# A graph network on one core: in the edge-maximum passes, every fourth block of edges comes by products with one-hots instead of every fifth

## What is computed

```python
def _sage_pool_layer(x, src, dst, Wp, bp, Ws, Wn, b, n_nodes):
    m = jax.nn.relu(x @ Wp + bp)
    msgs = m[src]
    agg = jax.ops.segment_max(msgs, dst, num_segments=n_nodes)
    agg = jnp.where(jnp.isfinite(agg), agg, 0.0)
    return x @ Ws + agg @ Wn + b
```

## Time and profile before

| | |
|---|---|
| median of 3 runs | 2809.11 us (2801.65 to 2812.70) |
| the profiled execution | 2804.64 us, its span 2802.9 us |
| first maximum pass, GpSimd's part | 663 to 1173 us |
| second maximum pass, GpSimd's part | 1246 to 1762 us |
| propagation (L2405) | 2000 to 2796 us |

### The profile page before, as it was taken

One profiled execution on the slowest core, in us unless ns is written; L12 is line 12 of the kernel. 1 busy time (PEld: TensorE's weight loads), 2 busy tenths in 40 slices (PEclk: granted clock), 3 DMA queues, 4 the chain that ended last, 5 costly groups with the idle time before them and its releaser, 6 DMA issues. The chain is left out here.

```text
span 2802.9 us, 72099 instructions
## 1 busy us (share of the span) xinstructions
PE 2456.9 (88%) x29232; PEld 1982.7 (71%) x29232; DVE 1763.4 (63%) x4833; ACT 1156.4 (41%) x2585; POOL 1299.8 (46%) x1607
## 2 busy tenths in 40 slices
PE   6998999986879888677889887469899999999999
PEld 3666777764556555445556655369899999999998
DVE  6997999986778877446768776320444444444444
ACT  5997888874434444424434444310311111111110
POOL 4007999974888888558888887410000000000000
PEclk8558999997999999789989998569999999999999
DMA  5103000013555555534545555549200000000000
GB/s 165 42 2 102 12 13 13 13 50 97 143 124 141 137 131 135 126 96 122 130 117 150 128 137 143 146 161 348 84 2 2 1 2 2 2 2 2 2 2 19
DMA packets 147170, 227.40 MB, mean 81 GB/s; under 512 B 55568, under 2 KB 112619, under 8 KB 146162
## 3 DMA queue, kind: packets, MB, share of 16 engines
q1 hardware_dynamic: 120350, 184.69, 22.0%
q0 software_dynamic: 22944, 36.72, 6.7%
q10 hardware_dynamic: 3540, 1.30, 0.2%
HBM read 122.26 MB, written 100.35 MB: 79 GB/s over the span
## 5 line engine op out<-in xcount | busy, mean ns | idle before, releaser
L1892 POOL DMA_INDIRECT max_row<-table,max_src_rows x640 | 670.5, 1048 | 181.7 <-issue 165.9
L1934 PE MATMUL max_far<-adj 128*96 128x512 f16 x1800 | 538.6, 401 | 7.7 <-issue 5.8
L2060 DVE TENSOR_SCALAR adj<-adj,node_numbers 128x512 f16<-128x512 f16 x900 | 325.0, 370 | 210.8 <-PE max_far L1934 129.2
L1758 POOL TENSOR_SCALAR e<-e 128x512 f32<-128x512 f32 (+1 forms) x625 | 365.7, 604 | 178.5 <-ACT e L1746 160.9
L2405 PE MATMUL prop<-g,adj 128*128 128x192 f16 x4608 | 387.2, 247 | 8.5 <-DVE g L2479 8.5
L1772 DVE TENSOR_TENSOR e<-e,a_ps 128x1024 f32<-128x1024 f32 (+1 forms) x313 | 372.3, 1195 | 32.6 <-PE a_ps L1684 12.6
L2405 PEld LDWEIGHTS prop<-g,adj 128*128 128x128 f16 x4608 | 380.7, 98 | 13.4 <-issue 9.2
L2405 PE MATMUL prop<-weights_then_states,adj 128*128 128x192 f16 x4608 | 384.3, 246 | 0.0
L2405 PEld LDWEIGHTS prop<-weights_then_states,adj 128*128 128x128 f16 x4608 | 378.9, 98 | 3.7 <-issue 2.5
L1746 ACT ACTIVATE e<-s_ps 128x512 f32<-128x512 f32 (+1 forms) x625 | 335.5, 585 | 60.2 <-PE o_ps L1696 37.8
L2513 DVE SCALAR_TENSOR_TENSOR support_parts<-prop,coef,weights_then_states 128x96 f32<-128x96 f32 x384 | 120.6, 314 | 303.9 <-PE prop L2405 226.0
(11 more groups left out here) (292 smaller groups left out, 3702.5 us busy)
## 6 DMA issues: line engine op xcount, KB each, us to landing
weights_then_states<-weights SPq DMA_DIRECT2D x100, 400.0 KB, 4.8
weights<-max_rows_w SPq DMA_DIRECT2D x52, 400.0 KB
rows_dram<-max_out SPq DMA_DIRECT2D x100, 192.0 KB
weights<-adj SPq DMA_DIRECT2D x48, 400.0 KB
max_same<-same_dram SPq DMA_DIRECT2D x196, 96.0 KB
rows_dram<-adj SPq DMA_DIRECT2D x96, 192.0 KB
max_row<-table,max_src_rows POOLq DMA_INDIRECT x640
adj<-ids_dram SPq DMA_DIRECT2D x36, 128.0 KB
```

Of the source, the lines that this page charges most:

```text
L1758: nc.gpsimd.tensor_scalar(e_tile(u), e_tile(u), math.exp(10.0), math.exp(-10.0), ALU.min, ALU.max).then_inc(clipped, 1)
L1892: nc.gpsimd.indirect_dma_start(row[i % RING][:, j, :], None, table_dram, bass.IndirectOffsetOnAxis(ap=src_rows[:, 4 * n + j:4 * n + j + 1] ...
L1934: mm = nc.tensor.matmul(far_ps[j % 2][0:D, :], parts[:, k, a, :], hot[(T * j + k) % HOTS], start=k == a == 0, stop=k == T - 1 and a == 1)
L2060: nc.vector.tensor_scalar(hot[i % HOTS], ids[j % 2], numbers[:, k:k + 1], None, ALU.is_equal).then_inc(hot_made, 1)
```

## The change

`FAR` is `range(4, 92, 4)` instead of `range(5, 92, 5)`. The far blocks are now 4, 8, ... 88: 22 instead of 18, and 76 near blocks instead of 80. Nothing else is edited; all that follows comes from loops over `FAR`, `near` and `far_tiles`.

```diff
 AWAY, NEAR_END = 5, 3
 
-FAR = range(5, 92, 5)
+FAR = range(4, 92, 4)
 
 K_PROP = 16
```

## The result

The changed kernel takes 2777.2 us as the median of four runs (2772.0 to 2783.7), beside 2805.5 us for the kernel before in those comparisons; the ratio is 0.9897 with a 95% interval of 0.9874 to 0.9920. It is faster by 1.0%, some 28 us. The forecast was 2801 us, no measurable change. The time lies inside the stated range, 2773 to 2831 us, which was wide enough to hold every rival, and within 4 us of the first rival, "GpSimd keeps its speed" (2781 us). The profiled execution has a span of 2770.3 us, 32.6 us less than before.

A forecast was written before the change was run, and what follows sets the result against it. GpSimd's queue was taken to bound both maximum passes. Per pass, -21.1 us of gathers, +13 of one-hot contention and +4 through TensorE gave -4, so -8 us for both: 2801 us, range 2773 to 2831.

The forecast's parts named there:

- GpSimd keeps its speed: Rival for both passes: added one-hots cost GpSimd only 7.2 us, nothing comes from TensorE; -28 us, 2781 us; chance 0.30.
- The bound: Both maximum passes: GpSimd's queue sets their length, about 5.2 us a step, while TensorE keeps up.
- Gathers removed: GpSimd's queue: 16 gathers fewer a pass, all of it counting; 21.0 and 21.2 us, -42.2 us for both passes.
- One-hots added: 100 more on VectorE a pass slow GpSimd's gathers and hots; 13 us a pass, between 7.2 and 17.6.
- the flat end: Lower bound of GpSimd's slowing by added one-hots, from thin stretches to the whole-pass rate; 7.2 us a pass.
- The steep end: Upper bound of GpSimd's slowing by added one-hots, from the whole-pass rate to two dense stretches; 17.6 us a pass.
- What comes through from TensorE: 42 us more TensorE work a pass thins its reserve and makes GpSimd wait; 4 us a pass taken.
- Sum: Both passes: -21.1 + 13 + 4 = -4 us a pass, -8 us in all, giving 2801 us.
- TensorE becomes the bound: Rival for both passes: 59 us of TensorE's idle time doesn't shrink; a pass 515 us, +22 us, 2831 us; chance 0.20.
- The port is held for whole one-hots: Rival: each added one-hot holds GpSimd 0.317 us, 31.7 us a pass; +21 us, 2830 us; chance 0.07.

The follow-up runs named there:

- gathers alone: Kernel before with four near blocks (16 gathers) a pass not gathered and nothing added; ratio 0.9878, -34 us.
- matmuls alone: Kernel before with 192 far matmuls more a pass, no gather less and no one-hot more; ratio 1.0017, +4.8 us.
- the repeat: The changed kernel (22 far blocks) run once more, on one chip beside the one with far blocks at 5, 9, ... 89; ratio 0.9915 to the kernel before.
- hots-only run: Kernel before with 100 one-hots more a pass into a spare buffer that nobody reads; ratio 1.0041, +11.5 us.
- hot on VectorE: First hot of each step made by VectorE instead of GpSimd; against the kernel before, 22, 18 and 13 far blocks: 2666.9, 2677.1, 2722.7 us.
- the alternating distance: Far blocks by turns four and five apart (20), first hots made by VectorE, against the kernel before; 2800.5 us, ratio 0.9978.
- other phase: The changed kernel with far blocks at 5, 9, ... 89 instead of 4, 8, ... 88; ratios 0.9915 and 0.9930 to the kernel before.

## Why the prediction was right and wrong

**The bound was right.** GpSimd's queue set both passes before and after. It fell from 509.6 to 496.0 us and from 514.4 to 500.5 us (first hot to last gather), -13.6 and -13.9 us, and the runs with gathers alone and matmuls alone show the same from two sides: the one moved the time, the other hardly.

**Gathers removed: right on the queue.** 16 x 1.311 = 21 us a pass. The fixed price is again about 0.26 us each. Alone, though, the removal gave 34 us in all (29 to 40), and 42 lies outside that interval; what took the other 8 us is open.

**One-hots added: the step that failed.** I took 13 us between 7.2 and 17.6. In the changed kernel the gathers cost 304 x 26 = 7.9 us more in the first and 304 x 37 = 11.2 us in the second pass; the first hots 1.3 us more and 6.0 us less. That is 9.2 and 5.2 us, 7.2 on average; the same sum from the trace of the repeat (gathers of 1073 and 1075 ns, hots of 829 and 831 ns) is 9.6 and 6.9 us. That one-hots cost GpSimd time was right, the size was the flat end's. The steep end came from two stretches in which TensorE and VectorE were catching up and all of VectorE's work was dense, a reservation that I named and then gave too little weight. How much of the 7.2 us the one-hots themselves cost is not settled: the gathers-only run has gathers 4.7 us a pass longer with none added, and the hots-only run puts 100 of them at 5.8 us. Two of the sums are slightly off, without weight: 62 ns of the hots scaled by 0.24 of 0.64 are 23 ns and not 26, and TensorE's 3.9 us a step with 2.5 matmuls of 0.22 us more are 4.4 to 4.5 us, not 4.3 to 4.4.

**What comes through from TensorE: too high.** I took 4 us a pass. GpSimd's waits went from 8.8 to 6.8 us in the first and from 6.6 to 12.2 us in the second pass; the matmuls-only run says 4.8 us for both passes together.

**Sum.** -21.1 + 7.2 + 2 = -12 us a pass against the -13.6 and -13.9 us on the queue; the fixed price fell by 4.0 and 7.7 us, 1.5 us a pass more than the 16 gathers' share, which is the rest. The passes themselves fell by 16.5 and 14.5 us, since the last scan now follows GpSimd's end sooner in the first pass (5.3 us instead of 7.4) and the second starts somewhat nearer. Where I wrote -8 us, the profile has -31 us in the passes of -32.6 us in all. Of the miss of 10 us a pass on the queue (-13.8 instead of -4), 6 us are the one-hots, 2 us what came through from TensorE and 1.5 us the fixed price; some 2 us a pass more lie at the ends of the passes. The first of these is the one that turned "no measurable change" into a gain of 1%.

**The rivals.** "GpSimd keeps its speed" is nearest to what happened, at 2781 us forecast and 2777 measured. Its own working, -13.9 us a pass, is met to within 0.3 us on the queue. Some of that closeness is luck: its sign was gathers of 1.06 us, and they took 1.072 and 1.086, the second nearly the 1.09 of the forecast; in the second pass 6.0 us less on the first hots and the smaller fixed price made up for 11.2 us on the gathers and 5.6 us more of waits. "TensorE becomes the bound" did not come. I had the idle time the wrong way round: the 31 us ahead of the turning of rows were to vanish and the other 59 us to stay. 20.5 of the 31 us stayed (in the first pass), and of the 59 us some 29 are left (487.5 - 438.4, less the 19.1 and 1.4 us ahead of the turning of rows; the 1.4 us are its idle time under "issue"), and TensorE's busy time rose by 25 and 20 us where 42 us of work at the full level were added. The clock gave part of that back: mean clocks of 0.94 and 0.93 that became 0.95 and 0.96 mean some 12 and 32 us less at the 1.2 GHz level, worth half of that if TensorE was busy in them, 6 and 16 us of the missing 17 and 22 (an estimate from the two windows, some 5 us either way). The rest is open, as in the matmuls-only run. At 30 blocks TensorE does become the bound, but by its work, with 9.7 us idle, and not by idle time that stays, which was this rival's mechanism. "The port is held for whole one-hots" is refuted by the one-hots-only run: 0.06 us for each, where the shortest lasts 0.317 us. By the rule of the Trainium skill, "SBUF — State Buffer", section "Who interferes with whom", the other engine is fully blocked for the whole of a VectorE instruction in a two-port mode. The runs show longer gathers beside more one-hots, but a price in time of a fifth of a one-hot. That need not contradict the rule: no run here shows the mode in which the one-hots run, nor for how much of a gather GpSimd would need the port. But the rule gave no usable price.

**Order of the signs.** The sense of the terms was right, and so was the warning that they would nearly cancel. I let the most likely case be the one in the middle of my bounds, and the queue followed their lower end. The rows of the whole pass (450 one-hots, GpSimd hardly waiting) should have counted for more than two stretches of 29 and 30 us.

## What to carry to other kernels

Look for the engine that hardly ever waits, not for the busiest: a queue of many small instructions with a fixed gap ahead of each (here 0.26 us) can set a stage at 80% busy, and "issue" idle time of nearly constant length is part of its price. Then ask of everything in that queue whether another engine can do it: four blocks moved gave 1.0%, the 100 small hots that nobody had questioned gave 3.8% on top. When such a queue is relieved, not all of the sum comes: taking 42 us of gathers off it gave 34 us, and taking 85 us of hots off a pass gave 56, because waits that the long queue had hidden came in.

## What the runs showed of the hardware

- In passes in which TensorE was idle less, its mean granted clock was higher: 0.99 with 9.7 us idle (30 blocks), 0.98 with 14 us (22 blocks, hot on VectorE), 0.96 with 48 us, 0.94 with 90.6 us, 0.91 with 94 us (13, hot on VectorE). Adding work to TensorE cost less busy time than its matmuls at the full level (25 and 20 us for 42 us in the changed kernel), of which the clock explains a part. The kernel with the alternating distance is the exception to be explained: 0.92 with 74 us, though GpSimd waits for TensorE in it.
- A GpSimd instruction that issues an indirect DMA took 1019 ns on average in a pass with 325 one-hots (13 far blocks, hot on VectorE) and 1132 ns in one with 750 (30 far blocks). In the three kernels of one comparison with the hot on VectorE it took 1019, 1033 and 1070 ns with 325, 450 and 550 one-hots. Passes with equal numbers of one-hots differ too: with 550 it took 1072 to 1094 ns in the traces of the changed kernel and its other phase.
- Idle time of TensorE that the profile puts under "issue" can go with results that are late, or reported late: in the kernel with the alternating distance a copy that waits only for `lay_out` started 6.7 us behind its recorded end, around 4.7 us of such idle time.
